# Layer 1's row maxima: band masks applied by predicated copies on VectorE

## The reference

```python
def _local_attention(q, k, v):
    ...
    dist = q_pos[:, :, None] - k_gpos[:, None, :]
    allowed = (dist > 0) & (dist <= w) & (k_gpos[:, None, :] >= 0)
    scale = 1.0 / np.sqrt(hd)
    scores = jnp.einsum('bhnqd,bhnkd->bhnqk', qb, kb) * scale
    scores = jnp.where(allowed, scores, NEG)
    attn = jax.nn.softmax(scores, axis=-1)
    ...
```

## Time and profile before

| | us |
|---|---|
| median of 3 runs (1736.76 to 1743.93) | 1740.39 |
| the profiled execution | 1738.24 |
| its span in the profile | 1736.4 |
| PE busy over the span | 1347.3 (78%) |
| DVE busy over the span | 968.2 (56%) |
| ACT busy over the span | 633.2 (36%) |

### The profile page before, as it was taken

One profiled execution on the slowest core, in us unless ns is written; L12 is line 12 of the kernel. 1 busy time (PEld: TensorE's weight loads), 2 busy tenths in 40 slices (PEclk: granted clock), 3 DMA queues, 4 the chain that ended last, 5 costly groups with the idle time before them and its releaser, 6 DMA issues. The chain is left out here.

```text
span 1736.4 us, 25416 instructions
## 1 busy us (share of the span) xinstructions
PE 1347.3 (78%) x9117; PEld 863.7 (50%) x9117; DVE 968.2 (56%) x2245; ACT 633.2 (36%) x1201; POOL 292.6 (17%) x278
## 2 busy tenths in 40 slices
PE   4578788888888887605999489888888888888753
PEld 2244544454545455405998345555555555554522
DVE  4365555555555566232777355767665766675632
ACT  0033333333333444303554124344444443435332
POOL 2110110011010100052111322213131313111210
PEclk9798999999999999856999589999989999999975
DMA  3441315142513130093221234304040404030000
GB/s 118 113 113 44 92 44 127 49 115 60 130 45 93 31 84 14 2 361 95 72 71 40 76 101 116 99 19 116 20 116 20 116 20 117 20 95 14 2 13 13
DMA packets 70924, 130.45 MB, mean 75 GB/s; under 512 B 7936, under 2 KB 60816, under 8 KB 67344
## 3 DMA queue, kind: packets, MB, share of 16 engines
q1 hardware_dynamic: 67728, 120.42, 25.3%
q0 software_dynamic: 3072, 8.41, 1.8%
HBM read 84.19 MB, written 43.81 MB: 74 GB/s over the span
## 5 line engine op out<-in xcount | busy, mean ns | idle before, releaser
L469 DVE TENSOR_REDUCE first_maxima<-bank 128x1 f32<-128x512 f32 (+3 forms) x352 | 220.8, 638 | 264.5 <-PE bank L305 263.5
L423 ACT ACTIVATE arena<-pair 128x512 f32<-128x512 f32 x320 | 184.8, 599 | 370.7 <-PE pair L330 369.1
L1420 DVE TENSOR_REDUCE second_maxima<-bank 128x2 f32<-128x512 f32 (+1 forms) x224 | 152.7, 685 | 191.8 <-PE bank L1133 190.7
L1288 ACT ACTIVATE second_probs<-pair 128x512 f32<-128x512 f32 (+1 forms) x256 | 137.5, 541 | 280.8 <-PE pair L1157 279.3
L304 PE MATMUL bank<-first_k_stack,first_q_stack 96*128 96x256 bf16 (+3 forms) x512 | 140.9, 309 | 39.5 <-DVE first_maxima L469 24.9
L284 PE MATMUL bank<-first_xT,w_qkv 128*128 128x512 f32 x256 | 133.7, 652 | 9.7 <-DMA first_xT<-in_xT 4.2
L329 PE MATMUL pair<-first_q_stack,first_k_stack 99*128 99x512 bf16 (+3 forms) x512 | 136.2, 305 | 1.6 <-ACT arena L423 1.1
L305 PE MATMUL bank<-constants_bf 128*128 128x128 bf16 x512 | 101.8, 224 | 0.0
L348 PE MATMUL pair<-arena,first_values 128*32 128x512 f32 (+3 forms) x1024 | 99.2, 506 | 1.4 <-ACT arena L423 1.4
L1154 PE MATMUL pair<-second_q_stack,second_k_stack 99*128 99x256 bf16 (+1 forms) x512 | 98.2, 276 | 2.6 <-ACT second_probs L1288 2.6
L536 POOL TENSOR_TENSOR first_halves<-first_halves 128x512 f32<-128x512 f32 x32 | 40.5, 1266 | 346.6 <-DVE first_halves L454 346.6
(11 more groups left out here) (311 smaller groups left out, 2538.1 us busy)
## 6 DMA issues: line engine op xcount, KB each, us to landing
parked<-first_parts SPq DMA_DIRECT2D x32, 384.0 KB, 2.8
first_q_stack<-parked SPq DMA_DIRECT2D x48, 256.0 KB, 4.8
first_k_stack<-parked SPq DMA_DIRECT2D x48, 256.0 KB, 7.8
parked<-second_parts SPq DMA_DIRECT2D x32, 384.0 KB, 2.5
second_q_stack<-parked SPq DMA_DIRECT2D x48, 256.0 KB, 5.1
second_k_stack<-parked SPq DMA_DIRECT2D x48, 256.0 KB, 7.9
sorted_x<-first_zero SPq DMA_DIRECT2D x3, 1670.5 KB, 12.4
expert_xs<-sorted_x SPq DMA_DIRECT2D x39, 128.5 KB, 2.3
```

Source lines behind the costliest of these rows:

```text
L423: act.activation(PT[:, s:s + len(heads), lo:lo + each], ex[n % 3][:, 0:len(heads) * each].rearrange("p (h q) -> p h q", h=len(heads)), ACT ...
L469: dve.tensor_reduce(nm[:, i, qt, heads[0]:heads[0] + len(heads)], mx[n % 2][:, 0:wide].rearrange("p (h k) -> p h k", h=len(heads)), AX.X, ...
L1288: act.activation(PT[:, s:s + len(heads), lo:lo + each], ex[n % 2][:, 0:len(heads) * each].rearrange("p (h q) -> p h q", h=len(heads)), ACT ...
L1420: dve.tensor_reduce(nm[:, i, qt, heads[0]:heads[0] + len(heads)], mx[n % 2][:, :].rearrange("p (h k) -> p h k", h=len(heads)), AX.X, ALU.m ...
```

## The change

- For the six two-head units of a group, the identity-with-mask matmul is left out. On DVE a predicated copy writes the scores of the tile before over those of the own tile, in PSUM, wherever the new constant `over` (1.0 where j >= i) is set: 2 x 128 elements a partition. Then, after a semaphore wait (`step`), the reduce goes over these 2 x 128 columns only. The seventh unit keeps its mask matmul and its reduce over 512 columns.
- The pair i = j = 0 is excluded by one more contraction row: row 96 of the q stack is -1e30 at each tile's first query and 0 elsewhere, row 96 of the k stack is 1 at each tile's first key and 0 elsewhere. Score matmuls take 97 rows instead of 96, exp matmuls 100 instead of 99, and the send goes to rows 97 to 99.
- Before the loop DVE fills these rows for both buffers with eight more memsets and two waits in between. PE's wait for `k_set` moves from its first exp unit to its first max unit.
- `over` (128 columns, f32) joins the late weights in `arena`.

```diff
         "bn_g": KC, "bn_b": KC, "bn_mean": KC, "bn_var": KC, "ln_g": KC, "ln_b": KC, "b_down": E1, "heads": LH,
-        "chunks": P // CH, "mS1": 2 * P, "mT1": 2 * P, "lat": NT * LAT}
+        "chunks": P // CH, "mS1": 2 * P, "mT1": 2 * P, "over": P, "lat": NT * LAT}
 ARENA = 7680
...
         lp = Loop(nc, ctx, ["x_ps", "pool_ps", "rkv_ps", "rq_ps", "rvr_ps", "ls_ps", "lt_ps", "r_ps", "qk_ps", "v_ps", "s_ps", "m_ps",
-                            "c_ps", "pv_ps", "o_ps", "a_ps", "y_ps", "z_ps", "rl_ps", "h_ps", "u_ps", "masks", "k_set", "v_set",
+                            "c_ps", "pv_ps", "o_ps", "a_ps", "y_ps", "z_ps", "rl_ps", "h_ps", "u_ps", "masks", "k_ones", "k_set", "v_set",
                             "h_set", "bn", "l_exp", "hi", "exps", "o_in", "g_exp", "z", "new", "r_exp", "near", "new2", "bd", "l_rec",
...
                         for r in range(3):
-                            sp.dma_start(QS[b % 2][ROWS + r:ROWS + r + 1, i * GH:(i + 1) * GH, :],
+                            sp.dma_start(QS[b % 2][ROWS + 1 + r:ROWS + 2 + r, i * GH:(i + 1) * GH, :],
                                           MS[r * GH:(r + 1) * GH, i % 2, :]).then_inc(lp[f"m_dma{i}"], 16)
...
                             pe.wait_ge(lp[f"stack{b % 2}"], 192 * (b // 2 + 1))
+                            if b == 0:
+                                pe.wait_ge(lp["k_set"], 1)
                         if n >= 2:
...
                             h = i * GH + hh
-                            pe.matmul(mx[n % 2][:, y * wide:(y + 1) * wide], q[0:ROWS, h, qt * P:(qt + 1) * P],
-                                      k[0:ROWS, h, k0:k0 + wide], start=(y == 0), stop=True, skip_group_check=True)
-                        pe.matmul(mx[n % 2][:, :], m["idb"][:, :], spread(mS[:, 2 * P - wide:2 * P], wide, len(heads)),
-                                  start=False, stop=True, skip_group_check=True).then_inc(lp["s_ps"], 1)
+                            ins = pe.matmul(mx[n % 2][:, y * wide:(y + 1) * wide], q[0:ROWS + 1, h, qt * P:(qt + 1) * P],
+                                            k[0:ROWS + 1, h, k0:k0 + wide], start=(y == 0), stop=True, skip_group_check=True)
+                        if qt == 0:
+                            ins = pe.matmul(mx[n % 2][:, :], m["idb"][:, :], spread(mS[:, P:2 * P], P, len(heads)),
+                                            start=False, stop=True, skip_group_check=True)
+                        ins.then_inc(lp["s_ps"], 1)
                     elif kind == "turn":
...
                             pe.wait_ge(lp[f"m_dma{i}"], 48 * (b + 1))
-                            if b == 0 and i == 0:
-                                pe.wait_ge(lp["k_set"], 1)
                         if n >= 2:
...
                             for kt in tiles:
-                                pe.matmul(ex[n % 2][:, lo:lo + width], k[0:KROWS, h, kt * P:(kt + 1) * P],
-                                          q[0:KROWS, h, kt * P:kt * P + width], start=(lo == 0), stop=True, skip_group_check=True)
+                                pe.matmul(ex[n % 2][:, lo:lo + width], k[0:KROWS + 1, h, kt * P:(kt + 1) * P],
+                                          q[0:KROWS + 1, h, kt * P:kt * P + width], start=(lo == 0), stop=True, skip_group_check=True)
                                 lo += width
...
                 for i in range(2):
-                    ins = dve.memset(KS[i][ROWS:KROWS, :, :].bitcast(i32), ONES)
+                    dve.memset(KS[i][ROWS:KROWS + 1, :, :].bitcast(i32), ONES).then_inc(lp["k_ones"], 1)
+                    dve.memset(QS[i][ROWS:ROWS + 1, :, :], 0.0).then_inc(lp["k_ones"], 1)
+                dve.wait_ge(lp["k_ones"], 4)
+                for i in range(2):
+                    dve.memset(KS[i][ROWS:ROWS + 1, :, :], 0.0).then_inc(lp["k_ones"], 1)
+                    dve.memset(QS[i][ROWS:ROWS + 1, :, :].rearrange("p h (t q) -> p (h t) q", q=P)[:, :, 0:1], NEG)
+                dve.wait_ge(lp["k_ones"], 6)
+                for i in range(2):
+                    ins = dve.memset(KS[i][ROWS:ROWS + 1, :, :].rearrange("p h (t q) -> p (h t) q", q=P)[:, :, 0:1], 1.0)
                 ins.then_inc(lp["k_set"], 1)
...
                         qt, heads = plan.MAX[j]
-                        dve.tensor_reduce(nm[:, i, qt, heads[0]:heads[0] + len(heads)],
-                                          mx[n % 2][:, :].rearrange("p (h k) -> p h k", h=len(heads)),
+                        low = mx[n % 2][:, :].rearrange("p (h k) -> p h k", h=len(heads))
+                        if qt > 0:
+                            step(dve.copy_predicated(low[:, :, P:2 * P], spread(w["over"].bitcast(u32), P, len(heads)), low[:, :, 0:P]))
+                            low = low[:, :, P:2 * P]
+                        dve.tensor_reduce(nm[:, i, qt, heads[0]:heads[0] + len(heads)], low,
                                           AX.X, ALU.max, negate=True).then_inc(lp["s_max"], 1)
...
     }
+    parts["over"] = j >= i
     parts["chunks"] = i // CH == np.arange(P // CH)[None, :]
...
         "b_rkv": x["L1_attn_rkv_b"].reshape(-1, 1), "b_down": rows(x["L1_ffn_b_down"].T),
-        **{k: const[k] for k in ("heads", "chunks", "mS1", "mT1", "lat")},
+        **{k: const[k] for k in ("heads", "chunks", "mS1", "mT1", "over", "lat")},
         **{k: chunks(x[f"L1_ffn_{k}"]) for k in ("bn_g", "bn_b", "bn_mean", "bn_var", "ln_g", "ln_b")},
```

## The result

| | before | after |
|---|---|---|
| median, us | 1742.16 | 1779.26 |
| runs, us | 1736.76 to 1756.98 | 1776.11 to 1780.69 |
| profiled execution / span, us | 1738.24 / 1736.4 | 1780.69 / 1778.9 |
| mean granted clock | 0.899 | 0.871 |

The ratio is 1.0197 [1.0132, 1.0261]: slower by 34 us by the ratio and by 37 by the medians, where 20 were forecast. The interval is wide, since one of the four runs before took 1756.98; over all 48 runs of the kernel before on record the median is 1740.0, and against that the change costs 39. The sign held, and so did the range of 8 in 10 (1738 to 1788). The forecast's own narrower range (1740 to 1775) did not, and two of the three terms did not either.

A forecast was written before the change was run, and what follows sets the result against it. PE was taken to set most of layer 1's pace, with DVE full in some stretches and the start a serial chain. Memsets +34.6 us, eight batches of copy +1.4 and masks -3.3 gave +19.4, so 1760 us; 8-in-10 range 1738 to 1788.

The forecast's parts named there:

- Part 3, the memsets: Layer 1's start on DVE: four new fills of 8192 bf16 elements delay PE's first matmul, +34.6 us once.
- The rival that the zero memsets cost half: Layer 1's start: two bf16 fit one written word, so +17.5 us instead of +34.6, total 1743; chance 0.16.
- Part 1, the mask matmuls: PE in layer 1: 192 of 224 mask matmuls go, at most 46 us; 3.3 us a batch come off the path.
- the other 15: Of 24 removed mask matmuls a batch, those where DVE waits for PE: 15 x 0.22 = 3.3 us gained.
- 9 of the 24 units: Removed mask matmuls a batch that lie ahead of PE's waits or where DVE is full; their gain becomes waiting.
- I take the full-clock price: Each removed mask matmul on PE counted at 0.22 us; the lower clock was taken to stand mostly behind long waits.
- POOL's next gathers stand behind its part of that chain: Layer 1's start: POOL's next gathers move with the delayed start chain; no separate size given.
- the five waits: PE's waits in one batch: zb 0.94 us, L1180 0.26, rest 1.08, mixed values 2.24, z 3.76; all said to involve DVE.
- Part 2, DVE per unit: DVE's maxima in layer 1: copy plus shorter reduce take 0.81 us instead of 0.61; seven units on the path, 1.4 us a batch.
- The sum: Whole kernel: +34.6 + 8 x (1.4 - 3.3) = +19.4 us, 1757.6 on the profiled execution, 1760 for the median.
- my signs for being wrong: Layer 1: the start moves by 17, the copy's row says 0.7, or a batch gets 4 us shorter or any longer.
- this rival: DVE becomes layer 1's bound if the copy takes two passes, +0.42 us a unit: +57 us, 1797; chance 0.17.

The follow-up runs named there:

- a2: The kernel before with only the 192 mask matmuls left out, reduce still over 512 columns: 1745.56 us, ratio 1.0024 to the kernel before.
- c1: The kernel before without the 192 mask matmuls, its gather's due time moved from 8.02 to 7.72 units ahead of its batch: ratio 0.9976 to the kernel before.
- b3: The kernel before with only the gather's due time moved from 8.02 to 7.72 units ahead of its batch: ratio 1.0046 to the kernel before.
- a3: The kernel before with its mask matmuls kept, plus the copy, the wait and the 256-column reduce on DVE: 1753.03 us, ratio 1.0062 to the kernel before.
- a1: The changed kernel with zero rows, -1e30 and 1.0 filled by POOL behind batch 0's gathers: 1768.29 us, ratio 1.0153 to the kernel before.
- a4: The changed kernel with the gather's due time moved from 8.02 to 7.72 units ahead of its batch: ratio 1.0164 to the kernel before.

## Why the prediction was right, and where it was not

**Part 3, the memsets: the mechanism right, the size wrong.** "four over a whole row of bf16: 16 x 512 = 8192 elements" was the failed step. They were written as 4096 uint32 words, so +18.3 us and not +34.6. The rival that the zero memsets cost half (+17.5) described this term; I had given it 0.16 against "nothing in the trace writes so". The Trainium skill (VectorE: DVE Perf Modes, on zero memsets issued as uint32) says that zeros over 2-byte elements can be issued as 4-byte words at half the elements. The rows of after agree: four fills of 8192 bf16 as 4096 uint32, 3.47 us each. One reading ahead of the sum was wrong as well: "The trace has only 4-byte memsets". The trace before has a small one of 128 bf16 ones (L608, 165 ns); it is not a zero, so it could not have shown the half cost either. Nothing covered the term, as said: PE's first matmul ends its wait with the casts behind the memsets.

**Part 1, the mask matmuls: the price right, the path wrong.** The 0.22 us each were PE's own. What failed is "in the other 15 DVE waits for PE again and again, so there 15 x 0.22 = 3.3 us a batch come off the path". That makes -26 us in eight batches; masks out alone measured +4. Two things that I had named took it. First, a PE that is sooner at its waits waits longer; I let this take 9 of the 24 units, but in a2's six periods, where 31 us of work are gone, the idle time grew by 18.4. With the gather shifted (c1) it grew by 10.9, so 7.5 of the 18.4 go with the third cause below. Secondly, "I take the full-clock price": the work that stayed got dearer: in the six periods, with their longer waits, the granted clock fell from 0.93 to 0.88, and PE's busy time lost 9.4 us instead of 31. The third was not named at all: "POOL's next gathers stand behind its part of that chain" was said of the start only, yet in four batches the gather that waits for the store holds up "mid" and "lo", and without the masks (a2, the change) "lo" then starts behind POOL's product and not ahead of it. That c1 gains 8 us by the shift that costs b3 as much shows this queue to be a part of the loss. How the remaining idle time and the lower clock share the rest is open. The reading of PE's waits also left one out: the five waits listed make 8.3 of the batch's 10.4 idle us, and the one of 0.94 us for x (1186.97) was among the missing. It ends with a DMA, not with DVE, and it grew most, to 3.13.

**Part 2, DVE per unit: right.** Copy 0.424 us (said 0.42), unit 0.80 (said 0.81), a3 +10.8 us (said 8 x 1.4 = 11.2, and 6 to 15 would have fitted), and no stall of the copy itself beside POOL. A stall was there, but on "lo" and in four batches only, and it is in a2, which has no copy, and not in a3, which has it.

**The sum.** +34.6 - 26 + 11 = +19.4 was forecast; the runs say +18.3 + 4 + 11 = +33. The two errors, 16 too much and 30 too little, partly cancelled, so it was partly luck that the wide range held. Of my signs for being wrong two came: the start moved by 18, which I had set down as 17, and a batch got longer (84.7 to 91.4). DVE did not become the bound: its share rose from 66% to 67% in the batch and from 65% to 68% in the six periods, where some 6 points were forecast; a3, with all of the copy and all of the masks, lost 11 us, not the 40 that this rival needed.

## What to carry to other kernels

Work taken from an engine that waits at fixed points of its order is worth only what the waits leave of it: try the removal alone first, since here 46 us less of PE's work gave nothing. An order with hand-set due times is tuned to the pace it was written for; when a change alters the pace, look at in-order queues that hold an item with an outside wait (here a gather behind a store), and move that item. One-off fills ahead of a stage's first matmul counted in full here, and moved to another engine they can come back as that engine's late next item.

## What was not expected of the hardware

- Beside a memset of 4096 words on POOL (two in 7.1 us), DVE's casts of 128 x 256 f32 to bf16 took 6.70 us for two and 3.68 for one instead of 0.50 and 0.29 (a1).
- "lo" on DVE, with two SBUF inputs, took 2.39 us instead of 0.63 where POOL's product of two SBUF tiles had started 0.07 us ahead of it. Where "lo" started 0.17 us ahead (before), it took 0.63 and the product 2.21 instead of 1.91: here the later of the two paid. In a4 "lo" is ahead again, at 0.63 to 0.69. The predicated copy, with one SBUF input and PSUM for the rest, took 406 to 430 ns in all 192 instances. The Trainium skill (SBUF — State Buffer, section "Who interferes with whom") says that a DVE instruction with at most one SBUF input, outside the two-port modes, does not contend with GpSimd, that one with two contends with a GpSimd instruction that reads SBUF, and that casts can take the shared ports; these three rows agree.
- A contraction of 97 rows instead of 96 left the cost of a score matmul as it was: the pair begins at 1202.73 and the next work at 1202.96, 0.23 us after 0.22:

```profile
1202.73 0.39 PE L1133 MATMUL bank<-second_k_stack,second_q_stack 97*128 97x256 bf16 x2
1202.96 0.38 PE L1156 MATMUL pair<-second_q_stack,second_k_stack 100*128 100x256 bf16 x2
```
